# Two-dimensional transform front of a fused mixer kernel: where the roots are computed, how far ahead the statistics run, one tile layout, the order of two transforms and of the loads

## The chip, the cores and the metric

The kernel runs on one core of a Trainium2 chip. The metric is the device time in microseconds (us). The kernel before took 1204.75 us (median of 3 runs, 1203.93 to 1208.91).

## What is computed

The input is x of shape (8, 64, 64, 64): batch, channel, height, width. Two layers follow each other, each a convolution block and a routed feed-forward block:

```python
x = x + conv0(ln_c(x))      # layer 0: spectral convolution
t = t + moe0(ln_t(t))       # tokens, 8 experts, top 2
x = x + conv1(ln_c(x))      # layer 1: depthwise 29 x 29 convolution
t = t + moe1(ln_t(t))
# conv0: Xf = fftn(X, axes=(H, W)); keep 32 x 32 modes; per mode a complex 64 x 64 matrix
#        over the channels; inverse transform; real part
```

`ln_c` subtracts the mean over the 64 channels and divides by sqrt(variance + 1e-6); `ln_t` does the same on tokens with 1e-5. The change lies in the first fifth of the program: ln_c of layer 0 and the forward transform.

## The kernel before

The program is written engine by engine. Each engine runs its own list in order, and semaphores tie the lists together; nothing is scheduled by a planner, so the order of the code is the order of the work.

**The front.** x lies in two layouts in HBM, 8 MB each: rows (`x_rows`, to tile X) for the statistics, and channels on the partitions (`x_chan`, to tile R1) for the transform. Both come in 4 pieces of 2 MB, on the queue of SyncE. For each piece VectorE takes statistics of 64 groups with `bn_stats` (L612) and computes 1/sqrt(variance + eps) by three Newton steps (`piece_root`, L545 to L568, 20 small instructions on 128x64).

The first transform runs over 32 column groups n, 8 for a piece. A group goes through four engines: TensorE multiplies 4 blocks of 128x128 in f32 with the cosine and sine table (L1192; the trace holds two records for each f32 matmul, 8 for a group) into one of 4 PSUM banks; VectorE multiplies by the root into one of 4 buffers `scaled` (L634); GpSimd adds the mean's share to the zero frequency (`centre_columns`, L388); ScalarE writes the f16 high part (L944); GpSimd writes the f16 low part, the difference (`c_dft_low_part`, L380). A bank is free after the VectorE step, a buffer after the low part.

The second transform has 16 groups, 12 or 15 f16 matmuls each (L1207), in the other 4 banks. ScalarE writes the high part (L954), VectorE the low part (L645), into tile xf2, in which the batch index is innermost. The order on every engine is: column groups 0 to 23, second transform 0 to 7, column groups 24 to 31, second transform 8 to 15. GpSimd clears two regions of R1 for the next stage in between (memsets, L398 and L400).

**What follows.** Mixing: for 18 rows of modes, two halves of a spectral matrix are loaded (L316), cut in f16 high and low parts by ScalarE (L982) and VectorE (L678), and multiplied on TensorE with two columns of xf2 (L1227, 128x16, 48 matmuls a row). Then two inverse transforms (L1282, L1379) and the token stage. The queue of SyncE loads the first matrices after column group 15, x in token order after the last statistics (L322), and narrow edge columns after the second transform (L325, L326); all later matrices wait behind these.

**Token stage.** 8 chunks of 32 token tiles a layer. The root of a chunk's variance starts on GpSimd (L412 to L420), gets its seed on ScalarE (`square_gap` L1023 and `root_seed`: Identity L1029, Ln L1030, Exp L1032), and is refined by one Newton step on GpSimd (L428 to L437). ScalarE then normalises 8 tiles at a time (L1047) and writes the high part (L1057), VectorE the low part (L721). There are 16 such roots, 8 a layer: three at each layer's start, five in its chunks. The compiler puts table loads for ScalarE's functions (ACT_TABLE_LOAD) in front of Ln and of Exp.

## Time and profile before

| | us |
|---|---|
| median of 3 runs | 1204.75 |
| the profiled execution, its own time | 1205.99 |
| its span, first to last instruction | 1204.2 |
| PE busy (x8490) | 912.3 |
| DVE busy (x2088) | 911.8 |
| POOL busy (x532) | 660.4 |
| ACT busy (x1163) | 576.0 |

PE is TensorE, DVE VectorE, ACT ScalarE, POOL GpSimd, SP SyncE. Busy times are those of the whole span; the front is its first 104 us. The 1.8 us between span and time lie outside the instructions.

### The profile page before, as it was taken

The page shows a single profiled execution, that of the slowest core. Times are in us where ns is not written, and L with a number is a line of the kernel's source. Part 1 is how long each engine was busy: PE and PEld are TensorE (multiplying, and loading weights), DVE is VectorE, ACT ScalarE, POOL GpSimd, SP SyncE. Part 2 cuts the span into 40 slices and gives each one's busy share as a digit, 9 for nine tenths or more (in the row PEclk, how much of TensorE's full clock was granted, in tenths as well). Part 3 has the DMA queues.
Part 4 walks back from the last instruction along what each step waited for, and adds up shares of the span by engine and source line. Part 5 has one row for each costly group of instructions (what it writes and reads, how often), then busy time and mean ns, then how long its engine had stood idle before and what let it go on. Part 6 is the DMA issues. An engine that isn't in the chain of part 4 may idle for free.

```text
span 1204.2 us, 24945 instructions
## 1 busy us (share of the span) xinstructions
PE 912.3 (76%) x8490; PEld 699.6 (58%) x8490; DVE 911.8 (76%) x2088; ACT 576.0 (48%) x1163; POOL 660.4 (55%) x532
## 2 busy tenths in 40 slices
PE   5964469776778777887369999999247887788887
PEld 5863468663445444554269999999124454445454
DVE  6978976677977788799956777754568788777884
ACT  1336854476655565530034444442576556555500
POOL 1542000325877687778474443310437777787787
PEclk9955579977889999999879999999559998899998
DMA  9865600010899992000358778883000000000000
GB/s 387 280 280 118 165 2 1 2 43 0 325 397 398 396 397 90 1 2 1 116 169 281 266 253 277 268 268 118 1 1 18 36 19 35 17 24 29 36 32 39
DMA packets 52865, 168.18 MB, mean 140 GB/s; under 512 B 13616, under 2 KB 13872, under 8 KB 51120
## 3 DMA queue, kind: packets, MB, share of 16 engines
q1 hardware_dynamic: 52784, 167.18, 39.3%
q8 instruction: 41, 0.67, 0.2%
q14 instruction: 40, 0.33, 0.1%
HBM read 98.68 MB, written 68.49 MB: 139 GB/s over the span
## 4 chain that ended last, share of the span: by engine, by line
PE 40%; DVE 24%; ACT 17%; issue 9%; POOL 6%; DMA 2%; ACTq 1%; DVEq 0%; SPq 0%; POOLq 0%
PE pair L1364 19%; ACT pair L1047 10%; DVE R L784 5%; PE pair L1332 5%; PE pair L1282 3%; PE pair L1329 3%; POOL R L458 3%; DVE R L829 3%; DVE work L612 2%; PE pair L1318 2%; PE pair L1319 2%; DVE R L721 2%; PE pair L1296 2%; DVE work L603 2%; ACT X L1081 1%
## 5 line engine op out<-in xcount | busy, mean ns | idle before, releaser
L784 DVE TENSOR_TENSOR R<-pair,R 128x1024 f32<-128x1024 f32 x256 | 310.0, 1215 | 96.7 <-PE pair L1319 90.6
L458 POOL TENSOR_TENSOR R<-R 128x1024 f32<-128x1024 f32 x128 | 304.4, 2378 | 123.1 <-DVE R L784 122.0
L1364 PE MATMUL pair<-R 128*128 (+4 forms) x2880 | 227.8, 243 | 21.6 <-DVE R L836 21.6
L1364 PEld LDWEIGHTS pair<-R 128*128 128x128 f16 x2880 | 224.9, 98 | 24.7 <-issue 22.0
L1318 PE MATMUL pair<-work,R 128*128 128x512 f16 x512 | 203.3, 397 | 35.6 <-DVE R L784 35.5
L1319 PE MATMUL pair<-work,R 128*128 128x512 f16 x512 | 201.2, 393 | 0.0
L1047 ACT ACTIVATE pair<-X,work 128x64 f32 (+1 forms) x496 | 168.8, 394 | 25.2 <-DVE R L721 20.0
L468 POOL TENSOR_TENSOR R<-R 128x512 f32<-128x512 f32 x128 | 163.1, 1274 | 11.3 <-POOL R L458 2.5
L845 DVE COPY R<-R 128x1152 f32<-128x1152 f32 x64 | 91.4, 1429 | 78.9 <-PE pair L1364 78.1
L1329 PE MATMUL pair<-X,ident_sb 128*128 128x256 f32 (+1 forms) x256 | 89.6, 434 | 76.3 <-ACT X L1081 67.0
L1332 PE MATMUL pair<-R,ident_sb 128*128 128x256 f32 x512 | 145.2, 410 | 0.0
L1081 ACT COPY X<-pair 128x256 f32 (+1 forms) x128 | 47.9, 374 | 202.2 <-PE pair L1332 202.2
L1107 ACT COPY R<-R 128x1152 f32<-128x1152 f32 x64 | 82.0, 1282 | 126.2 <-PE pair L1364 126.2
L1332 PEld LDWEIGHTS pair<-R,ident_sb 128*128 128x128 f32 x512 | 106.3, 208 | 17.2
L1318 PEld LDWEIGHTS pair<-work,R 128*128 128x128 f16 x512 | 51.9, 101 | 101.3 <-DVE R L784 59.2
L488 POOL TENSOR_TENSOR R<-X,R 128x1024 f32<-128x1024 f32 x16 | 46.8, 2922 | 111.1 <-DVE R L836 98.0
L1329 PEld LDWEIGHTS pair<-X,ident_sb 128*128 128x128 f32 x256 | 43.7, 197 | 106.1 <-issue 78.9
L1296 PE MATMUL pair<-ident_sb,R 128*128 128x128 f16 x512 | 43.5, 234 | 76.5 <-DVE R L721 49.4
L1296 PEld LDWEIGHTS pair<-ident_sb,R 128*128 128x128 f16 x512 | 34.6, 105 | 99.9 <-DVE R L721 82.8
L1319 PEld LDWEIGHTS pair<-work,R 128*128 128x128 f16 x512 | 51.8, 101 | 52.5 <-issue 10.0
L443 POOL TENSOR_TENSOR X<-X,R 128x512 f32<-128x512 f32 x4 | 5.1, 1274 | 125.1 <-ACT R L1120 125.1
L603 DVE BATCH_NORM_STATS2 work<-X 128x6 f32<-128x64 f32 (+1 forms) x512 | 72.1, 211 | 0.9 <-issue 0.7
(131 smaller groups left out, 1408.4 us busy)
## 6 DMA issues: line engine op xcount, KB each, us to landing
taps_halves<-R SPq DMA_DIRECT2D x128, 458.5 KB, 6.4
R<-taps_halves SPq DMA_DIRECT2D x64, 917.0 KB, 4.7
R<-spec_re SPq DMA_DIRECT2D x34, 256.0 KB, 4.1
X<-x_rows SPq DMA_DIRECT2D x4, 2048.0 KB, 20.9
R<-x_chan SPq DMA_DIRECT2D x4, 2048.0 KB, 25.3
X<-x_tok SPq DMA_DIRECT2D x4, 2048.0 KB, 13.9
out<-X SPq DMA_DIRECT2D x16, 512.0 KB, 2.6
R<-taps SPq DMA_DIRECT2D x2, 603.0 KB, 7.2
```

Source lines behind the costliest of these rows:

```text
L458: pool.tensor_tensor(h, pr[:, :, 0:256], pr[:, :, 256:512], ALU.add).then_inc(half_ready, 1)
L468: pool.tensor_tensor(w, h[:, :, 0:128], h[:, :, 128:256], ALU.add).then_inc(quarter_ready, 1)
L603: last = dve.bn_stats(stat[:, 32 * q + t, :], X[:, bass.ds(k * CT * C + t * C, C)])
L784: dve.tensor_tensor(pr.rearrange("p (k c) -> p k c", c=C), pair[p % 2][:, :].rearrange("p (k c) -> p k c", c=C), g.unsqueeze(2).to_broadca ...
L845: dve.tensor_copy(block_words(j, 0), band_words(i, 0)).then_inc(blocks_ready, 1)
L1047: last = act.activation(xn_psum[:, t * C:(t + 1) * C], X[:, bass.ds(k * CT * C + at * C, C)], ACT.Identity, bias=small[2 * q][:, at:at + 1 ...
L1296: mm = pe.transpose(out_[:, t * P:(t + 1) * P], parts[j][:, t * P:(t + 1) * P], ident16_sb[:, :])
L1318: pe.matmul(dst, u[q][:, t * P:(t + 1) * P], wa[:, 0:EC], start=True, stop=False)
L1319: mm = pe.matmul(dst, vh[q][:, t * P:(t + 1) * P], wb[:, 0:EC], start=False, stop=True)
L1329: pe.matmul(bank[7][:, 0:256], ident_sb[:, :], X[:, bass.ds(k * CT * C + g * 256, 256)], start=True, stop=False)
L1332: mm = pe.matmul(bank[7][:, 0:256], ident_sb[:, :], w[:, :, j, :], start=False, stop=(j == 1))
L1364: mm = pe.matmul(acc[:, y0:y1, x0:x1, :], blocks[i % 2][:, ks, 2 - y, 1 - x, :], src[:, y0 + y:y1 + y, x0 + x:x1 + x, :], start=(ks == 0 a ...
```

## The change

1. `piece_root` leaves VectorE. GpSimd does 10 small instructions and ScalarE 4 (Square, Identity, Ln, Exp) for each piece; one Newton step instead of three. The roots of pieces 1, 2, 3 are computed after column groups 3, 7, 15 (`ROOT_AFTER`).
2. VectorE takes the statistics of pieces 0 and 1 before its first column group, and those of 2 and 3 between groups 0 to 15, in two statistics tiles.
3. xf2 has the frequency innermost. VectorE's low part is one instruction for a group instead of two; TensorE's mixing matmuls read xf2 with a step of 34 elements.
4. After column group 24, each engine alternates: one column group, one group of the second transform.
5. For groups 17, 19, ... 31 VectorE computes the f16 low part instead of GpSimd (`low_by_vector`).
6. The loads have another order, the first row piece in two halves; the small constants move ahead.
7. ScalarE sets a table set by name at its start.

```diff
@@ sync
-            sp.dma_start(dft_sb[:, :], dft).then_inc(const_in, 16)
-            for i in range(NPIECE):
-                at = slice(i * PC, (i + 1) * PC)
-                sp.dma_start(X[:, at], x_rows[:, at]).then_inc(xr_in[i], 16)
-                sp.dma_start(xb[:, at], x_chan[:, at]).then_inc(xb_in[i], 16)
+            sp.dma_start(X[:, 0:half_piece], x_rows[:, 0:half_piece]).then_inc(first_in, 16)
+            sp.dma_start(X[:, half_piece:PC], x_rows[:, half_piece:PC]).then_inc(xr_in[0], 16)
+            sp.dma_start(dft_sb[:, :], dft).then_inc(dft_in, 16)
+            sp.dma_start(rank_sb[:, :], rank).then_inc(rank_in, 16)
+            sp.dma_start(X[:, piece(1)], x_rows[:, piece(1)]).then_inc(xr_in[1], 16)
+            sp.dma_start(xb[:, piece(0)], x_chan[:, piece(0)]).then_inc(xb_in[0], 16)
+            sp.dma_start(X[:, piece(2)], x_rows[:, piece(2)]).then_inc(xr_in[2], 16)
+            sp.dma_start(xb[:, piece(1)], x_chan[:, piece(1)]).then_inc(xb_in[1], 16)
...
-                    sp.wait_ge(ln_step, (NPIECE - 1) * LN_STEPS + 1)
+                    sp.wait_ge(piece_measured, NPIECE)
@@ gpsimd
+            def piece_root(i):
...
+                pool.wait_ge(piece_measured, i + 1)
+                step(0)
+                pool.tensor_tensor(total, stats[:, :, 1], stats[:, :, 4], ALU.add)
+                pool.tensor_tensor(gap, stats[:, :, 1], stats[:, :, 4], ALU.subtract)
+                pool.tensor_tensor(spread, stats[:, :, 2], stats[:, :, 5], ALU.add).then_inc(piece_step, 1)
+                step(2)
+                pool.tensor_tensor(spread, gap, spread, ALU.add).then_inc(piece_step, 1)
+                step(5)
+                pool.tensor_tensor(total, total, minus_half_c.to_broadcast([P, 64]), ALU.mult)
+                pool.tensor_tensor(t, seed, seed, ALU.mult).then_inc(piece_step, 1)
...
+            piece_root(0)
             for n in range(33):
                 if n < 32:
                     centre_columns(n)
-                if n == 0:
+                    if n in ROOT_AFTER:
+                        if n > 3:
+                            c_dft_low_part(n - 1)
+                        piece_root(ROOT_AFTER[n])
+                        if n > 3:
+                            continue
+                if n == 0 or low_by_vector(n - 1):
                     continue
@@ vector
-            piece_stats(0, 0, 64)
-            piece_root(0)
-            for i in range(NPIECE):
-                for g in range(8):
-                    scale_columns(i, g)
-                    if i + 1 < NPIECE:
-                        piece_stats(i + 1, 8 * g, 8 * g + 8)
-                if i + 1 < NPIECE:
-                    piece_root(i + 1)
-                if i >= 2:
-                    h_dft_low_parts(i - 2)
+            piece_stats(0, 0, 32)
+            piece_stats(0, 32, 64)
+            piece_stats(1, 0, 64)
+            for n in range(32):
+                scale_columns(n)
+                if n < 16:
+                    piece_stats(2 + n // 8, 8 * (n % 8), 8 * (n % 8) + 8)
+                if n >= 18 and low_by_vector(n - 1):
+                    c_dft_low_part(n - 1)
+                if n >= 24:
+                    h_dft_low_part(n - 24)
+            c_dft_low_part(31)
+            for n in range(8, 16):
+                h_dft_low_part(n)
@@ scalar
+            act.preload_act_table_set("natural_log_exp_and_others")
+            act.wait_ge(rank_in, 16)
+            piece_seed(0)
+            for n in range(32):
+                c_dft_high_part(n)
+                if n in ROOT_AFTER:
+                    piece_seed(ROOT_AFTER[n])
+                if n >= 24:
+                    h_dft_high_part(n - 24)
@@ tensor
-            dft_over_c(2)
-            pe.wait_ge(const_in, 7 * 16)
-            dft_over_h(0)
-            dft_over_c(3)
-            dft_over_h(1)
+            for n in range(24):
+                dft_over_c(n)
+            pe.wait_ge(const_in, 5 * 16)
+            for n in range(24, 32):
+                dft_over_c(n)
+                dft_over_h(n - 24)
...
-                return lambda t: xf2[:, t, a, 2 * b:2 * b + 2, :].rearrange("p s b -> p (s b)")
+                return lambda t: xf2[:, t, a, :, 2 * b:2 * b + 2].rearrange("p b s -> p s b")
```

VectorE around column group 24. Before, as it stands between the third piece's column groups and the second transform (L612 statistics, L634 scaling, the L54x and L55x rows the root):

```order
L634 TENSOR_TENSOR R<-pair,work 128x272
L612 BN_STATS work<-X 128x6 x8
L545 TENSOR_TENSOR work<-work 128x64
L546 TENSOR_TENSOR work<-work 128x64
L547 TENSOR_TENSOR work<-work 128x64
L549 TENSOR_SCALAR work<-work 128x64
```

Now, the stretch at column groups 23 to 27 (L694 scaling, L701 the low part of the first transform, L709 that of the second):

```order
L694 TENSOR_TENSOR R<-pair,work 128x272 x2
L701 TENSOR_TENSOR R<-R 128x68x4
L709 SCALAR_TENSOR_TENSOR R<-pair,R 128x4x68
L694 TENSOR_TENSOR R<-pair,work 128x272
L709 SCALAR_TENSOR_TENSOR R<-pair,R 128x4x68
```

The root's instructions are gone from VectorE, and the two low parts stand between its scalings.

GpSimd after column group 3. Now (L451 adds the mean's share, L425 to L442 are the root, L411 the low part); before, L388 and L380 simply alternate here:

```order
L451 TENSOR_TENSOR R<-R,work 128x8
L425 TENSOR_TENSOR work<-work 128x64
L426 TENSOR_TENSOR work<-work 128x64
L427 TENSOR_TENSOR work<-work 128x64
L429 TENSOR_TENSOR work<-work 128x64
L431 TENSOR_TENSOR work<-work,rank_sb 128x64
L432 TENSOR_TENSOR work<-work 128x64
L434 TENSOR_TENSOR work<-work 128x64
L436 TENSOR_TENSOR work<-work,rank_sb 128x64
L440 TENSOR_TENSOR work<-work 128x64
L442 TENSOR_TENSOR work<-work 128x64
L411 TENSOR_TENSOR R<-R 128x68x4
```

Ten instructions now stand between the mean's share of group 3 and the low part of group 2.

ScalarE at the first root of the token stage. Before (L1120 copies a PSUM bank for GpSimd, L1047 normalises):

```order
L1023 ACTIVATE work<-work 128x32
L1029 ACTIVATE work<-work,rank_sb 128x32
L1030 ACT_TABLE_LOAD
L1030 ACTIVATE work<-work,rank_sb 128x32
L1032 ACT_TABLE_LOAD
L1032 ACTIVATE work<-work 128x32
L1120 COPY R<-pair 128x512
```

Now, the same place:

```order
L1110 ACTIVATE work<-work 128x32
L1116 ACTIVATE work<-work,rank_sb 128x32
L1117 ACTIVATE work<-work,rank_sb 128x32
L1119 ACTIVATE work<-work 128x32
L1207 COPY R<-pair 128x512
```

The two table loads are gone here, and at each of the other 15 roots; one load at the start of ScalarE's list is the only one left.

## Rows read from the trace of the kernel before

**Rows 1.** The chain of waits, 0 to 170 us: start us, us, what

```profile
8.76 8.21 DVE work L612 x64
...
21.06 0.24 DVE work L568
...
69.18 5.33 DVE R L645 x8
...
75.58 13.73 PE pair L1192 x64
...
93.12 10.52 DVE R L645 x16
```

**Rows 2.** Groups by line and form, 0 to 110 us: count | busy us, mean ns | idle before

```profile
L612 DVE BATCH_NORM_STATS2 work<-X 128x6 f32<-128x64 f32 x256 | 34.6, 208 | 8.8 <-DMA X<-x_rows 8.8
L380 POOL TENSOR_TENSOR R<-R 128x272 f16<-128x272 f32 x32 | 28.2, 882 | 0.0
L944 ACT CAST R<-R 128x272 f16<-128x272 f32 x32 | 21.4, 669 | 56.2 <-POOL R L388 56.2
L645 DVE SCALAR_TENSOR_TENSOR R<-pair,R 128x136 f16<-128x136 f32 x24 | 15.7, 974 | 3.4 <-ACT R L954 3.3
L634 DVE TENSOR_TENSOR R<-pair,work 128x272 f32<-128x272 f32 x32 | 13.8, 435 | 7.9 <-PE pair L1192 6.9 <-POOL R L380 0.9
```

**Rows 3.** Busy time in two stretches (us; matmuls, loads, then granted clock)

```profile
22.00:26.00 4.00, 4.00 (x20) 4.00 (x20) 4.00 (x28) 2.00 (x3) 2.20 (x6) 1.00 1.04 446
75.60:78.00 2.40, 2.40 (x13) 2.40 (x13) 2.40 (x6) 0.48 (x1) 0.00 (x0) 0.50 0.99 423
```

**Rows 4.** Timeline: start us, us, engine, line; idle before and releaser in brackets

```profile
13.81 7.07 PE L1192 MATMUL pair<-dft_sb,R 128*128 128x68 f32 x32 [13.81 <-DMA dft_sb<-dft]
...
59.45 3.03 PE L1207 MATMUL pair<-dft_sb,R 128*128 128x68 f16 x51
```

**Rows 5.** Timeline around 64 us

```profile
64.25 0.94 POOL L380 TENSOR_TENSOR R<-R 128x272 f16<-128x272 f32 x1
64.36 0.96 DVE L546 TENSOR_TENSOR work<-work 128x64 f32<-128x64 f32 x1
```

**Rows 6.** Timeline, mixing stage

```profile
108.50 1.45 PE L1227 MATMUL pair<-R 128*128 128x16 f16 x48 [0.99 <-DVE R L678]
111.27 2.13 ACT L982 ACTIVATE R<-R 64x1024 f16<-64x1024 f32 x2 [2.88 <-DMA R<-spec_re]
120.87 2.46 DVE L678 SCALAR_TENSOR_TENSOR R<-R 64x1024 f16<-64x1024 f32 x2
```

**Rows 7.** Groups by line and form, ScalarE, whole span

```profile
L1030 ACT ACT_TABLE_LOAD x16 | 20.5, 1283 | 0.1
L1032 ACT ACT_TABLE_LOAD x16 | 20.5, 1283 | 0.3
```

**Rows 8.** Timeline, start of the token stage, layer 0

```profile
229.93 0.29 POOL L412 TENSOR_TENSOR work<-work 128x32 f32<-128x32 f32 x1 [1.68 <-DVE work L603]
234.87 0.24 POOL L428 TENSOR_TENSOR work<-work,rank_sb 128x32 f32<-128x32 f32 x1 [3.60 <-ACT work L1032]
235.32 3.12 PE L1379 MATMUL pair<-inv_c_sb,R 128*128 128x128 f16 x36 [3.31 <-ACT R L1120]
236.65 2.72 ACT L1047 ACTIVATE pair<-X,work 128x64 f32<-128x64 f32 x8 [1.38 <-POOL work L437]
...
259.05 0.69 DVE L721 TENSOR_TENSOR R<-pair,R 128x512 f16<-128x512 f32 x1 [0.61 <-ACT R L1057]
```

**Rows 9.** Timeline, later starts in both layers

```profile
275.50 0.69 DVE L721 TENSOR_TENSOR R<-pair,R 128x512 f16<-128x512 f32 x1 [2.43 <-ACT R L1057]
...
875.25 0.24 POOL L428 TENSOR_TENSOR work<-work,rank_sb 128x32 f32<-128x32 f32 x1 [5.26 <-ACT work L1032]
```

**Rows 10.** Timeline, one repeated chunk of layer 1

```profile
962.02 0.68 DVE L721 TENSOR_TENSOR R<-pair,R 128x512 f16<-128x512 f32 x1
962.94 2.71 ACT L1047 ACTIVATE pair<-X,work 128x64 f32 x8
```

224 lines of the change are left out of this document (133 added, 91 removed).

## The prediction

> **What bounds the kernel now.** I began with the page's busy shares and its chain of waits: no engine is over 76% busy, and the chain changes engine all the time, so a change is worth what it takes out of the chain where it stands. I then read the chain of the first 170 us [rows 1]. It is to be seen there that the front is a VectorE path: statistics of piece 0 alone (8.21 us), then a root whose last step ends at 21.3, three pieces of scaling and statistics, and the low parts of the second transform bare on the chain, 5.33 and 10.52 us, the last ending at 103.64. In between the chain is on TensorE for 13.73 us, eight column groups with nothing beside them. The groups by line [rows 2] give the prices: the 16 low parts are 32 instructions, 24 of them 15.7 us, 0.65 us for 136 elements, while VectorE scales 272 elements from PSUM in 0.435.
>
> The second view is the list of ScalarE's groups over the whole span [rows 7]: 32 table loads of 1283 ns, 41 us in all, two for each of 16 roots. The change names one table set for the whole program, and the new order has a single load. This is the part that works outside the front, so for each root I looked in the timeline at who waits behind it [rows 8 to 10].
>
> **The front, step by step.** *Start.* TensorE began at 13.81 [rows 4], when the table and the first channel piece were there. The new order puts a second row piece of 2.1 MB ahead of it; at 446 GB/s [rows 3] that is 4.7 us, so TensorE starts at about 18.7. Later pieces come every 9.5 us and are 14 us apart in use, so none is waited for again. VectorE does two pieces of statistics, 128 x 0.128 = 16.4 us, from about 6 (8.76 less half a piece, 2.4, is 6.4) to 22.4, and scales its first group then: 1.1 us later than at 21.3, with TensorE three groups ahead.
>
> *Root.* For 32 columns, GpSimd and ScalarE took from 229.93 to 236.65 [rows 8], 6.7 us with two table loads, so 4.1 without. For 64 columns I take 4.8. Root 0 (14.0 to 18.8) is hidden by the statistics of piece 1. Roots 1, 2 and 3 hold up GpSimd for 4.8 us while a column group needs 0.88 [rows 2] and some 0.2 more there, and TensorE delivers one in 1.72. Four buffers and four banks of slack, about 7 us, cover each of them; without that cover each costs up to 3 us. The first memset stands in GpSimd's list behind the backlog of root 3; I count it as covered as well.
>
> *TensorE's pace.* A column group took 7.07/4 = 1.77 us at 13.8 [rows 4] and 13.73/8 = 1.72 at 75.6 [rows 1]. The granted clock was 1.00 in one case and 0.50 (1.2 GHz) in the stretch of the other, with 0.20 and 0.18 us for a record [rows 3]: these f32 matmuls did not slow down at the lower level, so I price no clock here. 32 groups are 55 us: 18.7 + 55 = 73.7 if nothing is between. A group of the second transform took 3.03/4 = 0.76 [rows 4]; eight are interleaved, 6.1 us, to 79.8.
>
> *The ring.* From group 24 on, VectorE scales group n only behind the low part of n-25, so one round goes through four engines: scale 0.44 and high part 0.67 [rows 2], mean's share 0.2 (32 columns take GpSimd 0.24 in rows 8, this is 8), the high and the low part of the second transform 0.4 and 0.44 (both 272 elements out of PSUM, as the scaling is), five hand-overs of 0.05: 2.4 us, beside 1.72 + 0.76 = 2.48 on TensorE. Every other round has VectorE's new low part on top. That one I don't find in the trace. It is bounded below by the scaling's 0.44, above by two strided instructions, 2 x 0.65 = 1.3. I take 0.7, nearer the lower, since it has two SBUF operands and GpSimd works beside it: such an instruction of VectorE took 0.96 us at 64.36 and ended with GpSimd's of 64.25 [rows 5], where one of the same size took 0.24 [rows 1]. The Trainium skill ("SBUF — State Buffer", "Terms") calls the port pair of the two an exclusive lock held for the whole instruction; the row agrees. By that rule each such low part waits up to 0.9 us for GpSimd, 8 x 0.9 = 7 us if all stood on the path; in the ring only half of GpSimd's time is low parts, and I keep 0.7. Rounds of 2.5 + 0.35 from 61.7 (group 24 done): 8 x 2.85 = 22.8, so group 31's low part and with it the second half of the second transform start at 84.5.
>
> *End.* 8 x 0.76 = 6.1, to 90.6; ScalarE's high part 0.4, and its first half matrix 1.07 [rows 6], which used to be done beforehand: VectorE goes on at 92.1 instead of 103.64. Here 11.5 us are gained, of which 16 x (1.31 - 0.44) = 14 us is VectorE's cheaper low part. With 0.44 for the new low part as well it goes on at 91.4; with roots half as long again 95.5; if the low part of the second transform stayed at 1.31, 104, no gain.
>
> *Mixing.* It is paced by VectorE: 2.46 and one more low part, about 0.44, so 2.9 a row, against 1.45 for 48 matmuls [rows 6]. TensorE's new step of 34 elements costs nothing as long as a row stays below 2.9 us. The fourth matrix is requested when the first is cut, behind the edge loads in the queue; since VectorE no longer lags TensorE, these have a shorter start. ScalarE waited 2.88 for that matrix [rows 6]; I add 1.0 us, bounds 0 and 2.9. Front in sum: -10.5, between -13 and 0.
>
> **The table loads.** Each root loses 2.57 us of ScalarE. *Starts.* First root of layer 0: GpSimd waits 3.60 for the seed, TensorE 3.31 for a copy behind it, ScalarE 1.38 for GpSimd [rows 8]: all 2.57. Second: VectorE waits only 0.61 for what follows (259.05): 0.6. Third: VectorE idles 2.43 (275.50): 2.4. Layer 1: one such wait stands (GpSimd 5.26 at 875.25) [rows 9], and the other two of the three look like those of layer 0; VectorE is idle behind each: 7.7. *Chunks.* Ten roots. In the one shown, the normalising that follows at 962.94 needs VectorE's low part, which ends at 962.70 [rows 10], so only 0.24 us is to be had. The same pair of instructions, read at all ten, gives 0, 0.2, 0.1, 0.7, 0.7 in layer 0 and 0.7, 0.2, 0.2, 0.2, 0.2 in layer 1: 3.2. Sum 2.57 + 0.6 + 2.4 + 7.7 + 3.2 = 16.5, between 3 (a start's gain lost elsewhere) and 41 (all).
>
> The Trainium skill ("ScalarE: Activation LUTs", "What ACT_TABLE_LOAD costs") gives 1283 ns for a load, as measured here, and about 1.38 us of drain more for each switch. The 3.60 us of wait hold two loads (2.57) and three activations of some 0.3, with no room for two drains: the trace does not agree. By the page the starts' 6 roots would give up to 2.8 us more each, 1161 us at the end; chance 0.02.
>
> **Sum.** -10.5 - 16.5 = -27.0. The profiled execution has 1206.0 (span 1204.2 + 1.8), so 1179.0; from the median, 1.2 us lower, 1177.8. I forecast 1178 us.
>
> **Rivals.** *A, the other side: strided moving data.* TensorE reads 16 f16 elements with a step of 68 bytes in 918 matmuls. No row shows that. Now one takes 1.45/48 = 0.03 us. VectorE's strided f16 took 0.65/136 = 4.8 ns an element [rows 2]; at that price 16 are 0.077, a row 3.7 us: 16 rows lose 0.8 each over VectorE's 2.9, and the last 150 matmuls, bare, 7: +20, 1198. Slower than before by over 0.5% it is from 0.09 us a matmul on: 16 x (4.4 - 2.9) + 150 x 0.06 = 33 us, 1211. For it speaks only VectorE's price; against it that weights of 128 columns are loaded for 16 columns, so the moving side has slack. Chance 0.05 for some 1198, 0.03 for slower. The Trainium skill ("SBUF — State Buffer", "Door 1: The DMA port swizzle") states 16-byte lines and a penalty for each access on a new one; a step of 68 bytes meets one at every element. It gives no figure, and no run here shows it.
> *B, the root blocks GpSimd.* If the hand-overs are dearer on 64 columns, or the low parts wait for the port each time, the ring restarts late and the front gives 0 to 4: 1185 to 1189. For it: GpSimd gets 40 instructions more and is needed in each round; against: the slack of 7 us. 0.10.
> *C, the table loads were covered.* The chain passes through them, but the next wait may end last; then only the front counts: 1194. Against it stand the idle engines of rows 8 and 9. 0.06.
>
> **How the numbers follow.** The forecast, 1169 to 1186, has 0.72; B 0.10, C 0.06, A 0.05 and 0.03 for slower, the page's drain 0.02, and 0.02 for a change of nothing. The range 1169 to 1190 takes in B and leaves out under 2 in 10. Within 0.5% (6 us, about what a measurement can tell here) of 1204.75: 0.02; faster 0.95; slower 0.03.
>
> **What the profile after would show.** TensorE's first matmul at 18 to 19 us; 128 statistics in one run; column groups 1.72 apart up to 24; the second transform's low part at 0.4 to 0.5 us; the gap on TensorE before its group 8, some 5 us; the mixing's first VectorE step near 92; 48 mixing matmuls still in 1.45 us and rows 2.9 apart; one table load; the repeated chunks of the token stage hardly shorter. Wrong would be: low parts of 0.65 or more, mixing rows over 3 us, or a layer start as long as before.

## The result, and the profile after

The kernel after takes 1164.97 us (median of 4 runs, 1162.17 to 1167.92), the kernel before 1206.03 (4 runs, 1203.93 to 1208.91) on the same chip. The ratio is 0.966, 95% interval 0.9629 to 0.969. The gain is 41 us where 27 was forecast, and the time lies below the range.

The profiled execution took 1164.96 us, its span is 1162.8, the mean granted clock of TensorE 0.916; before it was 1204.2 at 0.886. Three rows of the page after (busy share of engines and clock in 40 equal slices, in tenths):

```profile
PE   3984579756887887787279999999157787878887
ACT  1448844475555555430044444443475555445510
PEclk9995579988989999999879999999569999899998
```

The slices with clock 5 are the mixing (the fourth and fifth slice) and the start of layer 1.

Where the 41 us came from is read by marks that both traces have: the start of the transposing matmuls behind the mixing (L1356 after), and ScalarE's exponential at L1163 (L1076 before), one in each token chunk. The third root of each layer stands behind that layer's first exponential, so of the 7.7 us forecast for layer 1's start 5.1 belong ahead of it and 2.6 to the first chunk.

| stretch | before, us | after, us | gain | forecast |
|---|---|---|---|---|
| up to the transposes | 164.84 | 155.21 | 9.6 | 10.5 |
| to layer 0's first exponential | 103.7 | 98.1 | 5.6 | 3.2 |
| to its second | 40.5 | 38.1 | 2.4 | 2.4 |
| layer 0, six more chunks | 232.6 | 226.2 | 6.4 | part of 3.2 |
| to layer 1's first | 338.8 | 333.2 | 5.5 | 5.1 |
| layer 1, first chunk | 38.0 | 34.8 | 3.2 | 2.6 |
| layer 1, six more chunks | 235.6 | 226.9 | 8.7 | part of 3.2 |
| rest | 50.2 | 50.2 | 0 | 0 |

The front and the end are close to forecast. The starts of the two layers gave 16.7 us for 13.3, the twelve chunks behind them 15.1 for 3.2.

**The front after.** Timeline rows (start us, us, engine, line; idle before and releaser in brackets):

```profile
19.06 5.36 PE L1277 MATMUL pair<-dft_sb,R 128*128 128x68 f32 x24 [19.06 <-DMA R<-x_chan]
34.00 0.44 DVE L694 TENSOR_TENSOR R<-pair,work 128x272 f32<-128x272 f32 x1 [2.25 <-POOL R L411]
30.97 0.29 POOL L431 TENSOR_TENSOR work<-work,rank_sb 128x64 f32<-128x64 f32 x1 [0.99 <-ACT work L1034]
85.18 5.11 PE L1292 MATMUL pair<-dft_sb,R 128*128 128x68 f16 x102 [4.88 <-issue]
91.75 3.72 DVE L746 SCALAR_TENSOR_TENSOR R<-R 64x1024 f16<-64x1024 f32 x3 [0.43 <-ACT R L1069]
```

TensorE began at 19.06 (forecast 18.7) and its second half of the second transform at 85.18 (84.5); VectorE's first half matrix came at 91.75 (92.1). Before, its first instruction starts at 103.24; the 103.64 of [rows 1], from which the prediction counts, is the end of the last low part, with which it overlaps. The gap of 4.88 before that second half is the one that was foretold, and a root (L431 waits only 0.99 for ScalarE) stops no one but VectorE, twice. The groups by line and form, 0 to 110 us (count | busy us, mean ns | idle before), answer to [rows 2]:

```profile
L680 DVE BATCH_NORM_STATS2 work<-X 128x6 f32<-128x64 f32 x256 | 33.9, 209 | 7.2 <-DMA X<-x_rows 7.2
L694 DVE TENSOR_TENSOR R<-pair,work 128x272 f32<-128x272 f32 x32 | 13.4, 427 | 8.2 <-POOL R L411 5.1 <-PE pair L1277 3.0
L709 DVE SCALAR_TENSOR_TENSOR R<-pair,R 128x272 f16<-128x272 f32 x12 | 5.2, 441 | 8.9 <-ACT R L1020 8.7
L701 DVE TENSOR_TENSOR R<-R 128x272 f16<-128x272 f32 x8 | 5.2, 650 | 7.5 <-ACT R L1012 7.5
```

The low part of the second transform is one instruction of 441 ns where it was two (group mean 974 with the waits inside), and VectorE's new low part takes 650 ns (0.7 forecast).

**The mixing after**, answering to [rows 6]:

```profile
99.28 1.60 PE L1314 MATMUL pair<-R 128*128 128x16 f16 x48 [0.94 <-DVE R L746]
102.40 2.13 ACT L1069 ACTIVATE R<-R 64x1024 f16<-64x1024 f32 x2 [2.44 <-DMA R<-spec_re]
103.49 2.47 DVE L746 SCALAR_TENSOR_TENSOR R<-R 64x1024 f16<-64x1024 f32 x2 [3.07 <-ACT R L1069]
```

A row's 48 matmuls take 1.56 to 1.62 us where they took 1.45: the strided moving read costs some 3 ns a matmul, hidden in rows that VectorE paces. The fourth matrix is waited for 3.07 us by VectorE, and of the 11.5 us won at the first half matrix (103.24 to 91.75) the front keeps 9.6 at its end.

**The roots.** ScalarE has one table load left, where the roots alone had 32 [rows 7]:

```profile
L1036 ACT ACT_TABLE_LOAD x1 | 1.3, 1283 | 0.8 <-PEq L1539 0.8
```

**The chunks.** Four chunks of layer 1, from exponential to exponential: two before, then a short and a long one after (columns: us, then busy us and count of PE, PEld, DVE, ACT, POOL, the granted clock, DMA share, GB/s).

```profile
1000.40:1041.40 41.00, 32.84 (x210) 19.93 (x208) 32.81 (x69) 23.36 (x61) 31.22 (x27) 0.92 0.06 26
1041.40:1082.30 40.90, 32.73 (x209) 19.91 (x208) 32.81 (x69) 23.25 (x60) 31.13 (x27) 0.92 0.06 26
```

```profile
923.10:960.60 37.50, 29.56 (x210) 18.17 (x208) 32.70 (x69) 20.77 (x58) 31.12 (x27) 1.00 0.07 29
1000.60:1041.20 40.60, 32.53 (x210) 19.94 (x208) 32.82 (x69) 20.81 (x59) 31.14 (x27) 0.92 0.06 26
```

This is the reading that the case turns on. The two chunks of after are one program with the same counts, ScalarE equally busy (20.8), and they differ by 3.1 us; TensorE's busy time differs by 3.0. The long one has a mean clock of 0.92, that is 2 x 0.08 x 40.6 = 6.5 us at the half level (1.2 GHz). The long chunk of before is no longer for its 2.57 us of table loads than a long one of after (41.0 and 40.6). Before, layer 1 had four chunks in a row of 41.0 at 0.92; after, two of 37.4 and 37.5, then 40.0, 40.6 and 38.8. Over all the chunks the same instructions of TensorE take less. Three rows of before (six chunks of layer 0, seven of layer 1, and the first of these seven by itself), and three of after:

```profile
309.10:541.70 232.60, 184.67 (x1251) 112.48 (x1250) 194.68 (x414) 130.33 (x331) 182.84 (x142) 0.97 0.66 255
880.40:1154.00 273.60, 214.49 (x1415) 130.54 (x1416) 214.78 (x415) 155.51 (x395) 203.47 (x163) 0.91 0.06 24
880.40:918.40 38.00, 23.32 (x166) 13.58 (x167) 28.14 (x68) 25.44 (x66) 21.21 (x22) 0.76 0.00 1
```

```profile
291.40:517.60 226.20, 182.76 (x1250) 111.51 (x1249) 194.53 (x414) 117.14 (x320) 182.63 (x143) 0.97 0.68 262
850.90:1112.60 261.70, 205.25 (x1415) 125.98 (x1416) 214.31 (x415) 139.95 (x383) 203.35 (x163) 0.95 0.06 25
850.90:885.70 34.80, 22.31 (x167) 13.18 (x168) 28.08 (x68) 22.67 (x64) 21.27 (x22) 0.81 0.00 1
```

TensorE's busy time falls by 1.9 and 9.2 us, of which 1.0 in layer 1's first chunk. So in the twelve chunks behind the starts it falls by 10.1, and as two chunks of one program differ by their busy time (3.1 and 3.0 us above), some 10 of the 15.1 us are clock.

In the chunks that repeat, a stretch at the half level begins where TensorE stands, or has just stood, idle for ScalarE's copy of a sum (L1081, now L1168). The same matmuls in both kernels, before at 1007.74 and after at 929.84:

```profile
1007.74 1.21 PE L1329 MATMUL pair<-X,ident_sb 128*128 x2 [1.86 <-ACT X L1081]
1008.75 1.91 PE L1332 MATMUL pair<-R,ident_sb 128*128 128x256 f32 x4
1010.46 0.63 PE L1318 MATMUL pair<-work,R 128*128 128x512 f16 x1
```

```profile
929.84 0.69 PE L1416 MATMUL pair<-X,ident_sb 128*128 x2 [1.77 <-ACT X L1168]
930.37 1.03 PE L1419 MATMUL pair<-R,ident_sb 128*128 128x256 f32 x4
931.23 0.38 PE L1405 MATMUL pair<-work,R 128*128 128x512 f16 x1
```

The idle time is nearly the same, 1.86 and 1.77 us, but the clock is 0.59 over the four microseconds from 1007 in one case and 1.00 behind the idle time in the other, and a matmul of 512 columns takes 0.63 or 0.38 us. So a chunk brings the occasion, and something else decides. Why TensorE stands is seen on ScalarE in the same chunk of before: the copy is queued behind eight normalising activations (2.71 us, from 1003.91) and a cast, and the next sum needs the bank that it empties.

```profile
1006.71 0.58 ACT L1057 CAST R<-pair 128x512 f16<-128x512 f32 x1
1007.19 0.38 ACT L1081 COPY X<-pair 128x256 f32 x1
```

### The profile page after: what moved, and what is told of

It is laid out like the page before. It is cut to its first block, busy times and chain, and to the rows that moved or that the text cites. A ratio compares the mean times of both kernels' runs of the same rounds, so it can differ in the third digit from the quotient of the medians.

```text
span 1162.8 us, 24889 instructions
## 1 busy us (share of the span) xinstructions
PE 897.7 (77%) x8490; PEld 692.3 (60%) x8490; DVE 885.7 (76%) x2004; ACT 538.2 (46%) x1147; POOL 667.2 (57%) x564
## 3 DMA queue, kind: packets, MB, share of 16 engines
q1 hardware_dynamic: 52928, 167.19, 40.6%
## 4 chain that ended last, share of the span: by engine, by line
PE 40%; DVE 21%; ACT 15%; issue 10%; POOL 8%; DMA 3%; ACTq 1%; DVEq 0%; SPq 0%; POOLq 0%
PE pair L1451 20%; ACT pair L1134 9%; DVE R L852 6%; PE pair L1419 4%; PE pair L1369 4%; PE pair L1416 3%; POOL R L529 3%; PE pair L1405 3%; PE pair L1406 3%; DVE R L897 2%; DVE R L789 2%; PE pair L1383 2%; DVE R L746 2%; DMA X<-x_rows 2%; DVE work L667 2%
## 5 line engine op out<-in xcount | busy, mean ns | idle before, releaser
L852 DVE TENSOR_TENSOR R<-pair,R 128x1024 f32<-128x1024 f32 x256 | 309.8, 1215 | 82.5 <-PE pair L1406 80.2
L1405 PE MATMUL pair<-work,R 128*128 128x512 f16 x512 | 200.8, 392 | 36.4 <-DVE R L852 36.3
L1406 PE MATMUL pair<-work,R 128*128 128x512 f16 x512 | 199.3, 389 | 0.0
L1416 PE MATMUL pair<-X,ident_sb 128*128 128x256 f32 (+1 forms) x256 | 87.1, 423 | 73.7 <-ACT X L1168 64.4
L1419 PE MATMUL pair<-R,ident_sb 128*128 128x256 f32 x512 | 139.9, 398 | 0.0
L1168 ACT COPY X<-pair 128x256 f32 (+1 forms) x128 | 47.9, 374 | 194.7 <-PE pair L1419 194.7
L1419 PEld LDWEIGHTS pair<-R,ident_sb 128*128 128x128 f32 x512 | 102.7, 201 | 15.6
```

The source lines that it names most:

```text
L852: dve.tensor_tensor(pr.rearrange("p (k c) -> p k c", c=C), pair[p % 2][:, :].rearrange("p (k c) -> p k c", c=C), g.unsqueeze(2).to_broadca ...
L1405: pe.matmul(dst, u[q][:, t * P:(t + 1) * P], wa[:, 0:EC], start=True, stop=False)
L1406: mm = pe.matmul(dst, vh[q][:, t * P:(t + 1) * P], wb[:, 0:EC], start=False, stop=True)
L1416: pe.matmul(bank[7][:, 0:256], ident_sb[:, :], X[:, bass.ds(k * CT * C + g * 256, 256)], start=True, stop=False)
L1419: mm = pe.matmul(bank[7][:, 0:256], ident_sb[:, :], w[:, :, j, :], start=False, stop=(j == 1))
```

## The experiments

### One half of the change alone

**e1_tables_only**: before, with the table set named at the start of ScalarE's list.

```diff
+            act.preload_act_table_set("natural_log_exp_and_others")
```

> The kernel before with one thing added: ScalarE sets the joint table set at its start, so the 32 table loads inside the roots go. The front is the old one. Theory S (slack): the loads themselves, by making ScalarE late, cause the half-clock stretches of TensorE in the token chunks; then nearly all of the gain behind the mixing stage (41.4 - 9.6 = 32 us of the profiled spans) comes here too: about 1174 us, and repeated chunks of layer 1 without a half-clock stretch, 37.4 us long. Theory D (direct, as predicted): only the waits that rows 8 to 10 show go: 16.5 us, 1188 us, chunks 40.8 us long. Theory P (phase): the stretches move with the moment at which a chunk begins; then anything between 1174 and 1192, with chunks of 37.4, 39 and 41 us mixed. The first mixing step of VectorE stays at 103.6 us in all three.

Measured: 1180.36 us (ratio 0.9838, 0.9789 to 0.9888): 24 us by the medians, 19.5 by the ratio, with an interval of 13.5 to 25.4 that holds my sum of 16.5. Its six runs lie in two groups, four at 1178 to 1181 and two at 1191 and 1194, so the whole time does not tell the sum from more. Its transposes begin at 164.94 as before, the first exponential at 263.7 (before 268.6). Layer 1's start is 333.3 long, as after. In layer 0 the chunks are nearly as before (40.6, 40.5, 42.8, 37.3); in layer 1 four read 37.2, 37.6, 37.4 and 36.7 at full clock, where before only the last had it. The starts' gain is real; the chunks' gain in this trace came in layer 1 alone, with the clock.

**e2_front_only**: after, without that line. Each root then loads tables again, 32 times in the token stage and 9 times in the front.

> The kernel after without the table set by name: every Ln and Exp has its table load again (16 roots of the token stage, and 4 roots of the front, 2.57 us each there). If the front's gain is separate: the first mixing step near 92 us plus what the longer roots cost the front (0 to 8 us), the token stage as before, so 1204.75 - 9.6 + 0 to 8 = 1195 to 1203 us. Theory S: chunks of layer 1 back at 41.0 us with two half-clock stretches. Theory P: they differ from both kernels, total down to 1185.

Measured: 1200.98 (0.9974, 0.9948 to 1.0001), hardly a gain. The mixing begins at 99.68, the transposes at 163.91: the front gives 0.9 us and not 9.6. The reason is in two views of this kernel. On GpSimd a root waits for the seed, on TensorE the column groups wait for the root:

```profile
33.52 0.29 POOL L431 TENSOR_TENSOR work<-work,rank_sb 128x64 f32<-128x64 f32 x1 [3.67 <-ACT work L1034]
...
37.05 8.80 PE L1276 MATMUL pair<-dft_sb,R 128*128 128x68 f32 x40 [0.83 <-DVE R L694]
49.47 13.93 PE L1276 MATMUL pair<-dft_sb,R 128*128 128x68 f32 x64 [3.62 <-DVE R L694]
66.35 3.68 PE L1276 MATMUL pair<-dft_sb,R 128*128 128x68 f32 x16 [2.95 <-DVE R L694]
```

3.67 against 0.99 after: 2.68 for two loads of 1283 ns. TensorE loses 7.4 us in three places. This is rival B, and what kept it away in the change is its last line: the roots fit on ScalarE only without the loads. The Trainium skill ("ScalarE: Activation LUTs", "What ACT_TABLE_LOAD costs") adds some 1.38 us of drain to each switch; 2.68 for two switches leaves 0.1 us for it, so the trace does not agree.

### Is it the moment at which a chunk begins?

**e3_late_layer1**: after, with 2.05 us of idle work ahead of layer 1's statistics.

```diff
+                    for t in range(16):
+                        dve.bn_stats(idle_sb[:, 6 * t:6 * t + 6], XV[:, 0, :])
```

> The kernel after, with 16 more statistics instructions (2.05 us, results unused) on VectorE just before those of layer 1, so that layer 1's chunks begin 2 us later and nothing else changes. Theory S: 1165 + 2 = 1167 us, and the chunks of layer 1 as in the kernel after: two of 37.5 us without a half-clock stretch, then 40.0 and 40.6. Theory P: the number of half-clock stretches in layer 1 changes, and the time with it by 2 to 3.5 us each: anywhere from 1160 to 1176.

Measured: 1174.3 (0.975, 0.972 to 0.978), 9 us more by the medians and 11 by the ratios, for 2 us of delay. Its six runs (1171.9 to 1178.46) all lie above the four of after (1162.17 to 1167.92). Two of its chunks in layer 1, and the six of layer 0:

```profile
893.30:933.50 40.20, 32.31 (x209) 19.80 (x208) 32.88 (x70) 20.71 (x58) 32.63 (x27) 0.92 0.07 27
933.50:974.30 40.80, 32.72 (x210) 19.85 (x209) 32.83 (x69) 20.78 (x58) 31.12 (x27) 0.92 0.07 27
292.20:523.00 230.80, 186.78 (x1251) 113.78 (x1250) 194.96 (x414) 117.20 (x321) 182.83 (x143) 0.96 0.66 256
```

The first two were 37.4 and 37.5 at full clock in after; the program of a chunk is untouched. But layer 0 runs ahead of the delay and is the same program as well, and in this execution its six chunks took 230.8 us where they took 226.2 in after, again with more busy time of TensorE (186.78 for 182.76). So the stretches also change from one execution to the next, by nearly 5 us here with no edit ahead of them. The chunks of one trace can't show what the delay did; the whole times can, and they say that a shift of 2 us at one place cost 9 to 11. That it did so by moving the moment at which the chunks begin is the reading that fits, and no run shows the rule.

**e10_copy_between**: after, with ScalarE's copy issued between the fourth and the fifth normalising activation, at pairs 5, 9 and 13.

```diff
                 for t in range(0 if by_pool else 8):
+                    if t == 4 and between:
+                        between()
...
-                        normalise(layer, k + 2, q, NORM_AT.index(p))
+                        normalise(layer, k + 2, q, NORM_AT.index(p), lambda: copy_at(p + 1))
```

> The changed kernel with one more edit: in the token stage ScalarE issues its copy of a sum of experts (0.38 us) between the fourth and the fifth of the eight normalising activations, at three places in a chunk, and no longer behind all eight and the cast. In the trace of the changed kernel TensorE idles 1.75 and 1.82 us at 967.35 and 958.67 for that copy, ten microseconds apart, and the half-clock stretches of a long chunk begin there. Theory P (the clock falls behind these idle times, in some chunks and not in others, by when the chunk begins): the two idle times shrink to under 0.6 us, every repeated chunk then has a mean granted clock of 0.98 or more, and each of the eleven takes 35 to 37.4 us; the six long ones of the changed kernel (38.1, 39.1, 39.8, 40.0, 40.6, 38.8) lose some 12 us together, and each of the others up to 1.5, so 1143 to 1156 us, and the spread of its runs is smaller than the 13 us seen before. Rival Q (the idle times have nothing to do with the clock, they are filled with other waits on ScalarE): chunks keep a length of 37.4 to 41.0 with stretches at 0.50, and the time stays within 1160 to 1172. Rival R (the copy moved forward delays the normalising, and the turn at the start of the next chunk waits instead): chunks of 38 and more at full clock, 1170 to 1180.

Measured: 1134.5 (0.939, 0.9364 to 0.9415), 30 us below after by the medians, 33 by the ratios: more than the best that was expected (1143).

```profile
290.70:503.60 212.90, 176.86 (x1251) 110.08 (x1250) 195.07 (x415) 116.27 (x319) 183.96 (x144) 0.99 0.72 280
835.60:1079.60 244.00, 199.12 (x1415) 123.94 (x1416) 213.50 (x415) 139.10 (x383) 203.27 (x163) 0.96 0.07 27
```

The chunks of both layers take 456.9 us for 487.9, and TensorE's busy time falls by 5.9 and 6.1: 12 us of clock. The other 19 are idle time of TensorE that was itself on the path: a chunk at full clock takes 35.1 to 36.8 and not 37.4, the sixth of layer 1 33.3. I had allowed up to 1.5 for each of the chunks without a stretch. The idle times did not shrink to under 0.6 us, as expected. The one of 1.82 us became two, for VectorE and then for the copy, and in place of the one of 1.75 TensorE waits as long for VectorE:

```profile
936.72 0.39 PE L1411 MATMUL pair<-work,R 128*128 128x512 f16 x1 [1.05 <-DVE R L852]
938.84 0.69 PE L1422 MATMUL pair<-X,ident_sb 128*128 x2 [1.09 <-ACT X L1170]
948.78 0.39 PE L1411 MATMUL pair<-work,R 128*128 128x512 f16 x1 [1.68 <-DVE R L852]
```

The clock is 1.00 all through this stretch, behind the 1.68 us too. A chunk of after at full clock has 7.9 us of TensorE's idle time in all, one of e10 6.0 to 7.1. Two chunks still hold a stretch (36.2 us at 0.96, 36.5 at 0.95), both at such a pair of waits. So less idle time goes with fewer stretches; a length of idle time from which the clock falls is not to be had from these traces.

**e12c_between_late**: e10 with the delay of e3.

> The kernel with the copy between the activations (1134.5 us) and a delay of 2.05 us (16 added statistics) ahead of layer 1's statistics. The same delay in the changed kernel cost 9 us (1174.3 against 1165.0), for layer 1's second to fourth chunk fell from 37.4 to 40.8. Theory P (what the delay cost there were stretches at half clock, which need TensorE's idle times of 1.8 us): here it costs its own 2 us, 1135 to 1139, and layer 1's chunks stay at 33 to 36.5. Rival P2 (the moment decides, idle times or not): a chunk of 38 or more in layer 1 and 1142 or more.

Measured: 1134.92 (0.9423, 0.9388 to 0.9459): 0.4 us over e10 by the medians, 4 by the ratios, whose intervals overlap. In after the same delay cost 9 or 11. One chunk of layer 1 did reach 38.4 (clock 0.95), which was expected only under P2, so single stretches still occur; none has two.

**e13c_before_between**: the edit of e10 on the kernel before, alone.

> The kernel before with the copy between the activations as its only edit; two table loads in each root stay. The ten repeated chunks took 38 to 42.6 us there, six of them with a granted clock of 0.92. Theory P: with TensorE's idle times gone the half-clock stretches go too, and a chunk takes 35 to 37, since a root's loads of 2.57 us then stand in ScalarE's slack: 1209 - 30 = 1176 to 1184. Rival T (in the kernel before the table loads themselves, 2.57 us of ScalarE in each chunk, bring the idle times of TensorE, and moving the copy doesn't help before they are gone): chunks at 39 and more, 1195 or slower.

Measured: 1159.95 (0.9633, 0.9598 to 0.9668): this one edit gives 43 us, as much as the whole change, and far more than the 1176 to 1184 expected. But for the first of layer 0 (39.7) and one of 41.8, its chunks take 33.4 to 36.7, with table loads in them (ACT 23.3 busy, 20.6 in e10):

```profile
938.00:974.20 36.20, 30.38 (x210) 18.72 (x208) 32.54 (x69) 23.27 (x60) 30.62 (x27) 0.97 0.08 31
974.20:1010.20 36.00, 29.97 (x211) 18.41 (x209) 32.04 (x68) 23.41 (x60) 30.29 (x27) 0.98 0.07 29
```

Between this kernel and e10 lies exactly the change, now with most of the stretches gone on both sides: 1159.95 - 1134.5 = 25.5 us, or by the ratios (0.9633 - 0.939) x 1204.75 = 29. The forecast was 27. The two come from different series, and the chunk of 41.8 holds an idle time of VectorE of 4.65 us that e10 lacks (it comes up again below), so the agreement is no closer than some 5 us.

**e14_between_13** and **e15_between_9**: e10's edit at one pair only, here against e10 for pair 13; for pair 9 the same with 10 and 9.

```diff
-                    if not (normed and p in (6, 10, 14)):
+                    if not (normed and p == 14):
...
-                        normalise(layer, k + 2, q, NORM_AT.index(p), lambda: copy_at(p + 1))
+                        normalise(layer, k + 2, q, NORM_AT.index(p), (lambda: copy_at(p + 1)) if p == 13 else None)
```

> The changed kernel with ScalarE's copy between the activations at one of the three places only, the normalising of pair 13 (in the trace of the changed kernel TensorE's idle time of 1.75 us that ends at 967.35). The copy at pair 9 (idle time 1.82, ending at 958.67) stays behind. Theory S1 (each of the two idle times brings its own stretch at half clock): a long chunk keeps the stretch behind the idle time of pair 9 and loses the other, so it takes some 39 instead of 41, a short one some 36.5 instead of 37.4, and the time lies midway, 1145 to 1155. Rival S2 (a stretch needs both idle times, ten microseconds apart): no chunk of layer 1 but its first over 37.5, 1138 to 1146. Rival S3 (one idle time is enough for both stretches): long chunks of 40 and more remain, 1157 to 1168.

> The mirror of the run before: the copy between the activations at pair 9 only, so TensorE's idle time that ends at 967.35 in the changed kernel stays and the one that ends at 958.67 goes. Theory S1: as there, one stretch left in a long chunk, the one behind pair 13, and 1145 to 1155. Rival S2: 1138 to 1146. Rival S3: 1157 to 1168. If the two runs differ by over 5 us, the two idle times are not alike.

Measured: 1157.01 (0.9635, 0.9582 to 0.9688) and 1155.11 (0.9606, 0.9555 to 0.9656). In the first no chunk of layer 1 but its first has a stretch, yet four of them take 36.7 to 37.4 and one 38.6; two of layer 0 do have one (38.7 and 37.6). In the second four of layer 1's seven have one.

```profile
920.70:958.10 37.40, 29.41 (x210) 18.09 (x208) 32.64 (x69) 20.70 (x59) 31.16 (x27) 1.00 0.07 30
```

```profile
917.80:956.10 38.30, 31.16 (x210) 18.88 (x208) 32.76 (x70) 20.88 (x58) 31.25 (x27) 0.96 0.07 29
```

No repeated chunk in either has two stretches (none of 40 us). None of the three theories fits both runs. By time S1 (1145 to 1155) is missed, narrowly by e15 and by 2 us by e14, which lies at the lower end of S3 (1157 to 1168), though S3's chunks of 40 are absent. By stretches e15 looks like S1 (38.3 and 38.0 with one, 36.7 and 36.6 without), and layer 1 of e14 like S2. In e14 the idle time of pair 9 stays at 1.82 us (ending at 956.13), with no stretch behind it. Taking one idle time away alone does not shorten a chunk at full clock (37.4 in e14: TensorE then waits 1.67 us for VectorE, L852, instead); taking both gives over 1 us. One profiled execution of each can't say more on which idle time matters.

### The parts of the front

Whole times here carry the token stage's stretches, so each is read by its stage. The six traces that share the front of after (after, e3, e10, e12c, e14, e15) have the first half matrix at 91.03 to 91.90 and the transposes at 154.68 to 156.13, so differences of up to 1.5 us between two single traces tell nothing.

| kernel | first half matrix | transposes | time, ratio |
|---|---|---|---|
| after | 91.75 | 155.21 | 1164.97, 0.966 |
| e4_edges_late | 92.28 | 158.10 | 1171.52, 0.9722 (0.9684 to 0.976) |
| e9_edges_last | 92.20 | 158.87 | 1172.1, 0.9724 (0.9681 to 0.9768) |
| e6_old_layout | 103.79 | 165.03 | 1187.19, 0.9832 (0.9798 to 0.9866) |
| e7c_low_on_pool | 89.87 | 154.42 | 1163.63 (median of three; a fourth took 1177.07), 0.967 (0.9598 to 0.9742) |
| e8_no_interleave | 87.91 | 151.85 | 1173.62, 0.9701 (0.9656 to 0.9745) |

**e4_edges_late**, **e9_edges_last**: the four edge loads behind the sixth and the thirteenth matrix.

```diff
+                if a == 5:
                     sp.wait_ge(h_dft, 16)
                     for r in BLOCKS:
                         sp.dma_start(edge_raw[r, 0], spec_re[:, 0:16, 16, :]).then_inc(edge_in, 16)
```

> The kernel after, with the four narrow edge loads issued behind the sixth matrix load instead of ahead of the fourth. If the narrow packets in the queue are what delays the fourth matrix (it landed 6.9 us after its issue, ScalarE waited 2.4 us and VectorE 3.1 us for it), the fourth matrix is cut 2 to 3 us earlier, and the mixing stage is 2.3 us shorter unless a later matrix then waits for the same packets: 1162.5 us. If the landing time is that of any transfer of this size, nothing changes: 1165 us. The time also contains what the shift does to the half-clock stretches later, so the mark is VectorE's first low part of the fourth matrix (103.49 us in the kernel after).

> The changed kernel with the four loads of the edge terms issued behind the thirteenth row of the mixing matrix and not behind the third. Behind the third they keep the fourth row away until 102.40 (ScalarE idles 2.44, VectorE 3.07 us); behind the sixth the fourth was there at 100.38, but ScalarE then idled 6.02 us for the seventh and the turn began at 158.1 against 155.2. Theory E (the loads of two-byte pieces hold the queue for some 5 us wherever they stand, and whoever is next pays what its buffers don't cover): the fourth row costs nothing (VectorE at 101.5), the rows of the stream stay 2.83 us apart, and the price comes at the fourteenth row or at the edge row itself, 1 to 4 us of idle; the turn begins at 153 to 156. Rival E2 (the price was only that of the place): nothing is waited for at all, and the turn begins at 152.0 to 152.8, 2.5 to 3 us earlier than in the changed kernel. The whole time is moved by the half-clock stretches of the token stage by up to 10 us either way under both, so the verdict is read from the stage.

They took the wait along: in e4 the fourth matrix was there at 100.38 instead of 102.40, and then ScalarE stood 6.02 us for a later one, or 7.55 in e9:

```profile
114.07 2.13 ACT L1070 ACTIVATE R<-R 64x1024 f16<-64x1024 f32 x2 [6.02 <-DMA R<-spec_re]
```

```profile
135.91 2.13 ACT L1070 ACTIVATE R<-R 64x1024 f16<-64x1024 f32 x2 [7.55 <-DMA R<-spec_re]
```

(The pieces are rows of 64 f32, 256 bytes, and not two bytes as the expectation has it.) Their place in the change, with 2.44 us of wait, is the cheapest of the three, where I had expected it to be the dearest.

**e6_old_layout**: after with the frequency outside, the low part in two strided instructions.

> The changed kernel with the transformed data in the layout of before (frequency outside, batch innermost), so that the low part of a group of the second transform is two strided instructions again, 32 in all and 16 extra; TensorE reads 16 contiguous elements in the mixing. Theory L (the layout carries the end of the front: 16 x (1.31 - 0.44) = 14 us, of which the part in the interleaved rounds is partly covered by TensorE): the second half of the second transform begins at 91.6 instead of 85.2, the first low part of the mixing matrix at 104 to 106 instead of 91.75, and the 48 mixing matmuls are back at 1.45 us from 1.6; the turn begins at about 155.2 + 12.5 - 1 = 166 to 168. Rival M (the interleaving alone hides the strided low parts): the first low part of the mixing at 92 to 95. Whole time 1165 + 12 = 1177, with up to 10 us either way from the half-clock stretches of the token stage.

The whole gain of the front goes: 103.79 and 165.03, as before. The layout carries it. The mixing is back at 1.43 to 1.45 us for 48 matmuls; from the fourth matrix to the transposes e6 takes 51.5 us and after 51.7, so that is worth nothing.

**e7c_low_on_pool**: all low parts of the first transform on GpSimd.

```diff
-            return n >= 16 and n % 2 == 1
+            return False
```

> The changed kernel with all low parts of the first transform on GpSimd: eight of 0.88 us more there, eight of 0.65 us less on VectorE. Theory V (VectorE's share of them is what keeps the rounds at the end of the first transform short): GpSimd, which has two memsets of 3.5 and 5.2 us and the last root in its list, falls behind, and the second half of the second transform begins at 86 to 90 instead of 85.18; the first low part of the mixing matrix at 92.5 to 97 instead of 91.75. Rival V2 (GpSimd has room for all, and VectorE gains its 0.65 a round): it begins at 84 to 85. Whole time 1165 plus the shift, with up to 10 us either way from the half-clock stretches of the token stage.

The second half of the second transform begins at 83.72 and not 85.18, the mixing 1.9 us earlier, 1.2 below the lowest of the six traces: GpSimd had room, and VectorE's eight low parts bring nothing. At the transposes the difference is within the spread. The whole time is the same within its interval.

**e8_no_interleave**: the first eight groups of the second transform in one run, on each engine.

```diff
+            for n in range(8):
+                dft_over_h(n)
             for n in range(24, 32):
                 dft_over_c(n)
-                dft_over_h(n - 24)
```

> The changed kernel with eight groups of the second transform in one run behind the twenty-fourth group of the first, and not alternating with groups 24 to 31; ScalarE and VectorE in the same order. Theory I (interleaving hides the second transform's high and low parts behind the first's groups): groups 24 to 31 then go at TensorE's 1.72 us, the ring of ScalarE (0.67 + 0.4) and GpSimd is no longer at its limit there, and the first eight groups of the second transform wait for banks at about 0.85 us each; in sum the first low part of the mixing matrix comes within 2 us of 91.75, at 90 to 94. Rival I2 (the alternating order is what carries the gain of the front): it comes at 96 or later. Whole time 1165 plus the shift, with up to 10 us either way from the half-clock stretches of the token stage.

The mixing begins 3.8 us earlier, more than either theory had: interleaving is a loss too. And yet the whole time is not shorter but 5 us (ratios) to 9 us (medians) longer than after's, at the edge of what the intervals tell, for four chunks of layer 1 fell to 40.1 to 41.0 and a fifth to 39.2.

### The version that the experiments point to

**e11c_both**: e8 and e10 together. **e16_both_pool**: with e7 as well.

> Two edits on the changed kernel: eight groups of the second transform in one run (alone it brought VectorE's first low part of the mixing matrix from 91.75 to 87.91 and the turn from 155.21 to 151.85, but the whole time was 1173.6 against 1165.0, with five of seven layer-1 chunks at 40 to 41 us and a granted clock of 0.92), and ScalarE's copy between the normalising activations (alone 1134.5). Theory P (the front's gain was lost because the token stage began at another moment, where its idle times brought half-clock stretches; with the idle times gone nothing is lost): the gains add, 1134.5 - 3.4 = 1131, between 1128 and 1134, each repeated chunk 33 to 37 us. Rival P2 (the shift also costs chunks without the idle times): 1138 or more.

> All that helped: the changed kernel with the copy between the activations at all three places, the first eight groups of the second transform in one run, and the low parts of the first transform all on GpSimd (alone this brought VectorE's first low part of the mixing matrix from 91.75 to 89.87). The two without the third took 1131.5. If the gains of the front add, that mark comes at 86 to 87 instead of 87.6 and the time is 1129 to 1131.5; rival: in one run the first eight groups hid behind GpSimd already (TensorE waited 3.37 us for its low part there), so that GpSimd with all of them is late, the mark comes at 88 to 91 and the time is 1132 to 1135.

1131.54 (0.939, 0.9354 to 0.9427) and 1130.23 (0.9393, 0.9348 to 0.9437). The first half matrix is at 87.58 and 87.95, so e7 adds nothing here. Both beat before by 6% and after by 33 to 35 us. One chunk of e11c took 38.7, over the 37 that was expected. By the medians they are 3 to 4 us below e10, by the ratios level with it: whether the front's gain is kept can't be told from these runs.

## Why the prediction fell short, step by step

- *Start, root, pace, ring, end of the front.* Right, within 1 us at each mark. The roots kept TensorE waiting for nothing, as said, though VectorE stood for them twice (2.25 and 2.87 us). But they were covered only because the loads went (e2): the two halves of the change are not a sum.
- *VectorE's new low part, edges, mixing.* 650 ns for 0.7; the fourth matrix came late by more than the 1.0 allowed, and the stage lost 1.9 us from the first half matrix on, 2.3 from the prediction's own mark of 103.64, both inside the bounds. The strided read (rival A) cost 3 ns a matmul and no time.
- *Starts.* Forecast 2.57 + 0.6 + 2.4 + 7.7 = 13.3, read 5.6 + 2.4 + 5.5 + 3.2 = 16.7. The term that was too small is the second root of layer 0, 0.6 us: the stretch with the first two roots gave 5.6, and 4.9 in e1, where nothing but the loads went. Layer 1's 8.7 for 7.7 holds 1.0 us of clock.
- *Chunks.* This is the step that failed. I took 3.2 us from the 0 to 0.7 us that the normalising could come forward, and gave the clock no term at all. Measured are 15.1. Of these some 10 are TensorE's same work at a higher clock. About 3 more belong to one chunk of layer 0, 42.6 us before and 37.3 after, in which VectorE once idled 4.64 us. The other kernels with the old front have that idle time too (e1 4.60, e13 4.65), none of those with the new one has it, so it went with the front; the trace names no cause for it, and no run looked for one. What is left, about 2, is near the term as it was forecast.
- *The view that would have told.* Before the change the chunks already read 37.3 and 37.9 at clock 1.00 beside 41.0 at 0.92, with equal counts. I read the clock only in the front, where f32 matmuls don't feel it, and never divided the chunks by their clock. Had I, the range would have reached down by up to 3.6 us for each of the six chunks at 0.92 or 0.93, 21 us.
- *Rival C* (only the front counts) falls with e1, 19.5 to 24 us without the front. The added drain, which had 0.02, falls with e2's 2.68 us.

That the clock's part of the surplus is not the change's own is argued from three runs. In e3 a delay of 2 us takes 9 of it back. Between e13 and e10, where most stretches are gone on both sides, the change is worth 25.5 to 29. And e8 wins 3.4 us in the front and loses 5 to 9 in sum. What decides whether a given idle time brings a stretch stays open. Of the 3.4 us more in the starts 1.0 is clock too; the rest is the change's own, a term of the sum that was too small.

## What to carry to other kernels

Where one repeated block of the same program has two lengths, read the granted clock of each: the difference is a term that any change ahead of it can win or lose, and it belongs in the range. One trace is not enough for that: the same chunks differed by nearly 5 us between two executions. Look for TensorE's idle time at the head of each stretch at half clock, and take it away at its source: here a copy of 0.38 us queued behind 2.7 us of work on another engine was worth more than the whole rewrite of the front. And a move of work to another engine has to be priced with what that engine does around it, here two table loads for each root.

## What the runs showed of the hardware

- TensorE's clock fell to 0.50 behind an idle time of 1.86 us in a chunk of before and stayed at 1.00 behind one of 1.77 in a chunk of after, the same matmuls. In e14 it stayed at 1.00 behind one of 1.82, in e10 behind one of 1.68; a delay of 2 us upstream (e3) cost 9 to 11 us in sum. A 512-column f16 matmul takes 0.63 us at the low level and 0.38 at the high one, while the f32 column groups of the front don't change [rows 3].
- Runs of one kernel spread widely: 12.5 us for before in one series (1200.35 to 1212.82), 15 over three runs of e7c; 4 in e10 and e12c, but 9 again in e11c.
- A matmul that read 16 f16 elements of moving data with a step of 68 bytes took 3 ns longer (1.60 for 1.45 us over 48); f16 results written by VectorE with a stride cost 654 ns for 136 elements [rows 2], contiguous 441 for 272.
- Four loads of 256 KB in rows of 256 bytes held the stream of matrices up by 2.4 to 7.6 us of ScalarE's wait, more the later they stood.
